# Attention phase of a ViT tower: row-maximum scores taken two steps ahead instead of one, and the work of a pair of images dealt anew over its six steps

## What is computed

```python
h = patches(x) @ W.T + b                      # 64 x 196 x 192
xn = layernorm(layernorm(h)) * g + beta
q, k, v = split(xn @ qkv_w.T + qkv_b)         # 12 heads of 16
attn = (q @ k.T) * 16 ** -0.5
attn = attn - 0.2 * (sum of the 8 neighbours of each element of attn)
h = h + softmax(attn) @ v
h = h + experts(layernorm(h))                 # top 2 of 8 experts
```

## Time and profile before

| what | value |
|---|---|
| median of 3 runs | 2177.81 us (2173.88 to 2178.31) |
| profiled execution | 2189.16 us, of which 2187.4 us from its first to its last instruction |
| attention phase | until about 1,240 us of the span |
| mean granted TensorE clock | 0.925 of full speed (2.4 GHz) |
| busy share over the span | PE 86%, DVE 67%, ACT 58%, POOL 53% |

### The profile page before, as it was taken

How to read it: one execution, slowest core, us unless ns; L and a number is a source line. 1 busy time by engine, 2 the same in 40 slices (tenths; PEclk the granted TensorE clock), 3 DMA queues, 4 the chain that set the end, 5 groups by cost and what they waited for, 6 DMA issues and landing times. The chain is left out here.

```text
span 2187.4 us, 54001 instructions
## 1 busy us (share of the span) xinstructions
PE 1891.2 (86%) x17949; PEld 1406.2 (64%) x17949; DVE 1461.1 (67%) x4652; ACT 1266.8 (58%) x2469; POOL 1152.0 (53%) x1069
## 2 busy tenths in 40 slices
PE   4758888888888989898888479999999999999991
PEld 3546666666666666666665256777777777777771
DVE  4658888888888888888887345655555555554440
ACT  3557788787878788787877323433434343333330
POOL 3335555555555545555552254666666666654452
PEclk7878999999999999999999559999999999999996
DMA  4564746666574747575664237787877878798876
GB/s 142 144 187 143 202 147 190 168 182 168 173 197 146 215 142 198 161 195 157 183 173 132 65 106 197 186 211 184 206 185 205 190 201 194 190 195 184 180 176 193
DMA packets 356572, 382.56 MB, mean 175 GB/s; under 512 B 138388, under 2 KB 319952, under 8 KB 352144
## 3 DMA queue, kind: packets, MB, share of 16 engines
q1 hardware_dynamic: 314768, 338.64, 55.3%
q0 software_dynamic: 41664, 42.12, 11.1%
HBM read 232.83 MB, written 135.46 MB: 168 GB/s over the span
## 5 line engine op out<-in xcount | busy, mean ns | idle before, releaser
L1838 ACT ACTIVATE mh<-mid_bank 128x512 bf16<-128x512 f32 x336 | 200.8, 598 | 464.0 <-PE mid_bank L1529 349.6
L824 DVE TENSOR_REDUCE row_max<-s_bank 98x2 f32<-98x392 f32 x768 | 396.6, 558 | 97.6 <-PE s_bank L607 94.7
L1750 DVE SCALAR_TENSOR_TENSOR ml<-mid_bank,mh 128x512 bf16<-128x512 f32 x336 | 231.6, 689 | 341.9 <-ACT mh L1838 333.7
L1020 ACT ACTIVATE probs<-t_bank 98x392 f32<-98x392 f32 x768 | 340.6, 498 | 42.1 <-PE t_bank L623 31.1
L1904 POOL DMA_INDIRECT sums<-y_out,tail x168 | 265.1, 1578 | 172.9 <-DVE y_out L1780 95.8
L1543 PE MATMUL y_bank<-wst,mh 128*128 128x192 bf16 x1344 | 330.0, 246 | 8.3 <-DVE y_out L1780 7.5
L1546 PE MATMUL y_bank<-wst,ml 128*128 128x192 bf16 x1344 | 330.1, 246 | 0.0
L1545 PE MATMUL y_bank<-wst,mh 128*128 128x192 bf16 x1344 | 329.8, 245 | 0.0
L623 PE MATMUL t_bank<-q_stack,k_stack 104*98 104x196 f16 x1536 | 248.6, 269 | 40.0 <-ACT probs L1020 25.5
L1193 POOL TENSOR_TENSOR x_lo<-x_buf,x_hi 128x588 f16<-128x588 f32 x128 | 188.7, 1478 | 170.6 <-ACT x_hi L1001 112.8
L1889 POOL DMA_INDIRECT slots<-row_r,spot x196 | 190.7, 973 | 98.0 <-issue 56.7
(11 more groups left out here) (236 smaller groups left out, 4515.7 us busy)
## 6 DMA issues: line engine op xcount, KB each, us to landing
wst<-packed SPq DMA_DIRECT2D x56, 1584.0 KB
x_buf<-in_x_t SPq DMA_DIRECT2D x32, 1176.0 KB, 9.0
q_stack<-stack_parts SPq DMA_DIRECT2D x96, 294.0 KB, 4.8
k_stack<-stack_parts SPq DMA_DIRECT2D x96, 294.0 KB, 6.7
stack_parts<-qk_hi SPq DMA_DIRECT2D x32, 588.0 KB, 2.9
stack_parts<-qk_lo SPq DMA_DIRECT2D x32, 588.0 KB, 2.8
sums<-h_buf SPq DMA_DIRECT2D x32, 294.0 KB
h_in<-sums SPq DMA_DIRECT2D x32, 294.0 KB
```

What stands on the lines that cost most here:

```text
L824: nc.vector.reduce_max(row_max[st.odd][:, :, hh:hh + 1], s_bank[hh % 2][0:HALF, :, 0:TOKENS], AX.X).then_inc(max_ready, 1)
L1020: nc.scalar.activation(probs[st.odd][:, hh], t_bank[hh % 2][0:HALF, :, 0:TOKENS], ACT.Exp).then_inc(probs_ready, 1)
L1750: nc.vector.scalar_tensor_tensor(ml[n % MID][:], mid_bank[n % MID_PS][:], 0.0, mh[n % MID][:], ALU.max, ALU.subtract).then_inc(ml_ready, 1)
L1838: nc.scalar.activation(mh[n % MID][:], mid_bank[n % MID_PS][:], ACT.Relu).then_inc(mh_ready, 1)
```

## The change

`scores`, `row_maxima` and `split_maxima` run two steps ahead (`LOOK = 2`); `transpose_max` and `copy_max_rows` stay one ahead, and so take maxima of the step before. The work of a pair is dealt anew: patches are multiplied in steps 0 to 2 instead of 1 and 2, and split one pair earlier; `project_v` has step 3 alone; `statistics` are in step 2, `statistics_n` in step 3, `inverse_deviation_n` in step 4; `layernorm_n` is in steps 0 and 1, `high_rows` in step 3 and `low_rows` in step 4 of the pair after the one where they were. The stacks are still made in six transfers, which the first scores of a pair wait for, now in step 4 of the pair before instead of step 5. The first two pairs are filled in interleaved, and the last pair drains over 12 steps instead of 7.

```diff
-DRAIN = STEPS + 1
+DRAIN = 2 * STEPS
+LOOK = 2
+FILL = 4
...
                 elif k == 0:
-                    load_x(Pair(body, kk, 2))
+                    load_x(Pair(body, kk, 3))
                     load_h(Pair(body, kk, -1))
-                    store_rows(Pair(body, kk, -2))
                 elif k == 1:
...
-                    for low in range(2):
-                        store_parts(Pair(body, kk, 1), low)
+                    store_parts(Pair(body, kk, 1), 0)
+                elif k == 2:
+                    store_parts(Pair(body, kk, 1), 1)
                     for low in range(2):
                         stack(Pair(body, kk, 1), low)
...
+                elif k == 5:
+                    store_rows(Pair(body, kk, -2))
...
             def step(body, kk):
-                if kk == -1:
+                if kk == -FILL:
                     fill_pipeline()
-                scores(Step(body, kk, 1), (0, 1))
+                scores(Step(body, kk, LOOK), (0, 1))
                 mix(Step(body, kk, -1))
                 transpose_back(Step(body, kk, -2))
                 scores_less_max(Step(body, kk, 0), (0, 1))
-                scores(Step(body, kk, 1), (2, 3))
+                scores(Step(body, kk, LOOK), (2, 3))
+                if kk >= 0:
+                    between_heads(body, kk)
                 scores_less_max(Step(body, kk, 0), (2, 3))
-                if kk >= 0:
-                    before_max(body, kk)
                 transpose_max(Step(body, kk, 1))
                 if kk >= 0:
-                    after_max(body, kk)
+                    after_heads(body, kk)
...
-                row_maxima(Step(body, kk, 1), (0, 1))
-                normalise(Step(body, kk, -2))
+                row_maxima(Step(body, kk, LOOK), (0, 1))
                 if kk >= 0:
...
                     elif k == 5:
                         split_low(Pair(body, kk, 2))
-                row_maxima(Step(body, kk, 1), (2, 3))
-                split_maxima(Step(body, kk, 1))
+                normalise(Step(body, kk, -2))
+                row_maxima(Step(body, kk, LOOK), (2, 3))
+                split_maxima(Step(body, kk, LOOK))
...
                 exponentials(Step(body, kk, 0), (0, 1))
-                if kk >= 0 and k < 2:
-                    high_patches(Pair(body, kk, 2), 2 * k)
+                if k >= 3:
+                    high_patches(Pair(body, kk, 3), k - 2)
+                elif k == 0:
+                    layernorm_n(Pair(body, kk, -2), (0, 1))
+                elif k == 1:
+                    take_high_tilde(Pair(body, kk, 1))
                 exponentials(Step(body, kk, 0), (2, 3))
+                copy_max_rows(Step(body, kk, 1))
...
                 elif k == 1:
-                    split_patches(Pair(body, kk, 2), (1, 2, 3))
+                    if Pair(body, kk, 1).there:
+                        pool.wait_ge(plain_lo_ready, Pair(body, kk, 1).u + 1)
                     sum_rows(Pair(body, kk, -1))
...
+                elif k > 3:
+                    split_patches(Pair(body, kk, 3), (k - 3,))
+                    if kk >= 0 and k == 4:
+                        inverse_deviation_n(Pair(body, kk, -1))
+                        low_rows(Pair(body, kk, -2))
```

More of the change, by code:

```diff
@@ L137, in run_bodies @@
 def run_bodies(eng, step):
-    step(0, -1)
+    for kk in range(-FILL, 0):
+        step(0, kk)
     for body in range(2):
@@ new lines, in fill_pipeline @@
+                pe.wait_ge(weights_in, 16 * len(LOADS))
+                pe.wait_ge(consts_set, CONSTS)
+                transpose_xn(first, 0)
+                transpose_xn(first, 1)
+                for c in range(2):
+                    project_patches(second, 0, c)
+                for i in range(BLOCKS):
+                    project_qk(first, i)
+                for c in range(2):
+                    project_patches(second, 1, c)
+                project_v(first, 0, (0, 1))
+                project_v(first, 1, (0, 1))
@@ L1007, in _ @@
             for i in range(2):
+                if i == 1:
+                    for tile in range(TILES):
+                        high_patches(Pair(0, 0, 1), tile)
                 for hh in range(HG):
```

217 lines of the change are left out of this document (110 added, 107 removed).

## The result

The changed kernel takes **2278.65 us** (median of 4 runs, 2277.55 to 2282.44), the kernel before, run again beside it, 2175.85 us (2169.55 to 2178.31): 1.048 times the time, 95% interval 1.0453 to 1.0507, or 103 us more. The forecast was 2217, at most 2275. The sign was right and the size was not.

What follows compares the result with a forecast made beforehand. Nearly full PE, DVE and ACT lose time in handing over; the change closes a loop through the stacks. Period 36.9 + 0.8 = 37.7 us, +62 over 26 periods, start -25, drain +2: +39, so 2217 us, range 2150 to 2275.

Steps and rivals of the forecast that it cites:

- The closed chain: Step 4's scores through steps 5, 0, 1, parts stored and stacks loaded to the next step 4: 36.9 us before the clock.
- 37.7 forecast: Period of a pair in the attention phase: 36.9 us of loop plus 0.8 for the clock, 2.4 more than now.
- the clock: PE's idle wait before step 4 brings half the clock, slowing step 4's matmuls: 0 to 1.6 us, taken as 0.8.
- the meeting at `split_low`: In step 5 POOL's low_rows delays DVE's split_low, so step 5 ends at 12.7 us after step 4's start, not 11.0.
- 3.0, 11.6 and 0.3: Way to the stacks: 2.9 plus 0.1 us to the first load, 11.6 of loads, 0.3 for low parts held up.
- The forecast had `sum_rows` meet `take_low_tilde` itself: sum_rows waits for take_low_plain, meets take_low_tilde and holds the low parts up by some 0.4 us: +0.3.
- it starts at 6.7 us, together with `split_low`: low_rows, behind a patch split that follows ACT's step 4 patch copy, starts 6.7 us after step 4's start; split_low at 6.8.
- All of it meets: Rival: both POOL operations between split_low's two, half clock through project_qk; period 39 to 40, at 39.5 2264 us; chance 0.12.
- an undisturbed pair: The pair whose step times the loop was summed from: 21.2 us from step 4's scores to the end of take_high_tilde.
- Together -25: The start: interleaved fill some 10 us sooner and the 17.45 us wait gone, -15; bounds -10 and -30.
- counted from the third pair on, not from the sixth: The longer period was charged from the sixth pair on: 26 periods, +62 us.
- +2: The longer drain of the last pair adds 2 us.

Runs made afterwards that it cites:

- e3: The changed kernel with its six stack loads cut into 18, six per group of four heads, step 4 waiting for its own group alone: 2218.85 us, ratio 1.021.
- e7: e6 with e4's edit, POOL's low_rows and step 5 patch split held until split_low is over: 2158.48 us, 0.988 of the kernel before.
- e8: The changed kernel with PE given 32 matmuls on the old stack, result unread, while it waits for the new one: 2308.00 us, ratio 1.054.
- e6: e3 with e5's edit, so 18 loads by group and normalise before split_low in step 5: 2215.36 us, ratio 1.013.
- e11: e6 with high_rows and low_rows in step 2, the packed weights' low parts earlier, and six whole stack loads again: 2239.39 us, ratio 1.033.
- e4: The changed kernel with POOL's low_rows and step 5 patch split held back until split_low has ended: 2276.50 us, ratio 1.048.
- e5: The changed kernel with DVE normalising before split_low in step 5: 2271.95 us, ratio 1.038.
- e1: The changed kernel with scores one step ahead instead of two (LOOK = 1), the new order kept: 2338.56 us, ratio 1.079.
- e14: e13 with scores one step ahead instead of two (LOOK = 1): 2460.03 us, 1.124 of the kernel before.
- e13: e7 with the low parts of the packed weights made earlier, in steps 3 and 4 instead of 5: 2158.55 us, ratio 0.986.

## Why the prediction was right and wrong

**Right.** The closed chain. Stacks are needed a step sooner, PE stands 3.3 to 3.7 us for them in front of step 4, the last landing comes 0.2 us before, and the loop's parts add up to the period. `max_parts` left PE's waits.

**Right by luck, the even pairs' sum.** 37.7 forecast, 38.1 measured, with step 4 at 5.7 us (forecast 4.3, and 0.8 for the clock), step 5 at 7.2 (8.4), step 0 at 4.8 (5.2), `take_high_tilde` at 4.4 (4.1) and 16.0 to the next scores (14.9). The 1.7 us of the meeting at `split_low` are in the forecast and not in the pair; what stands in their place is a longer step 4, 1.0 us at the maxima, and 1.1 on the way to the stacks. Of this last, the first load is issued 4.0 us behind `take_high_tilde`, at 763.18, right after the store of the low parts at 762.72, and the last lands 11.8 us later; I had 3.0, 11.6 and 0.3. The low parts are stored late because `take_low_tilde` starts only at 761.20, behind the maxima of step 1, and these meet POOL's `sum_rows`. DVE's timeline:

```profile
759.96 1.02 DVE L863 TENSOR_SCALAR max_parts<-row_max 98x8 f16<-98x8 f32 x1
```

And POOL's:

```profile
759.13 1.81 POOL L1239 TENSOR_TENSOR att<-att,h_in 98x768 f32<-98x768 f32 x1 [2.74 <-DVE att L882]
```

That row of DVE takes 1.02 us there in every pair from 300 to 1100 us, where it took 0.21 in the kernel before. The forecast had `sum_rows` meet `take_low_tilde` itself.

**Wrong, the meeting's place.** "it starts at 6.7 us, together with `split_low`". The forecast hung POOL's run on the patch copy that ACT makes in step 4. But POOL's split in step 4 takes the tile that ACT has copied in step 3, and so it starts as soon as POOL's layer norm of step 3 is over, in the changed kernel 0.36 us before the scores of step 4:

```profile
774.80 1.31 POOL L1224 TENSOR_TENSOR x_lo<-x_buf,x_hi 128x588 f16<-128x588 f32 x1
```

Counted from the scores that open step 3, `low_rows` starts after 12.1 us in the changed kernel (777.87 - 765.77) and after 12.2 in e3 (783.26 - 771.08). Step 4 comes 9.4 us behind step 3 with the wait for the stacks, and 5.6 without. So POOL works on while PE stands, and `low_rows` starts 2.7 us into step 4 in the changed kernel (777.87 - 775.16) and 6.6 us in e3 (783.26 - 776.64), where the forecast's 6.7 comes out by luck. The wait that I had put at the head of the chain I had not put between POOL and PE. So the run fell on the maxima of step 4, which it holds up by 2.7 us in the odd pair shown and by 1.0 in the even one. "All of it meets" at 39.5 us was the rival that came true in the odd pairs, on another row and with the half clock through `project_qk` that it had named; it had 0.12. What I had not listed at all is `pack`, a third operation in the run of every second pair; and the sum was taken from an undisturbed pair, whose step 5 took 6.06 us, while in every second pair of the kernel before it took 7.2 to 8.8. Period 39.2 instead of 37.7: 37 us over 26 periods.

**Wrong, the start.** "Together -25". The first scores came 9.6 us sooner (59.02 for 68.59), the 17.45 us wait is gone, and `take_low_tilde` of the third pair came 17.3 us sooner (117.8 for 135.1). By the sixth pair 0.8 was left. PE waited 7.83 and 4.82 us at the next two steps 4. The view names no releaser for these two waits; that they are for stacks is read from the place. In e3, where a group's scores wait for its own loads alone, they are 1.84 us and nothing, and the sixth `take_low_tilde` comes at 240.62, 10.2 us sooner than before (250.78); in e7 it comes 18.3 sooner. So the head start can't be kept when the loop through the loads is already closed, and the longer period should have been counted from the third pair on, not from the sixth: 3 x 3.9 = 11.7 of the 16.5 us that went between them. In all that is 24 us.

**The drain** was nearly right: "+2", and from the last `take_low_tilde` to the first matmul of the experts the changed kernel takes 0.9 us more (146.5 for 145.6). The other 9.6 us of the gain behind it lie in the expert phase, which the change doesn't touch and the forecast couldn't know.

37 + 24 - 1 - 10 = 50 us, and 89.8 - 39 = 51.

**The clock** can't be given a price of its own here. Step 4 took 5.7 and 4.9 us where part or all of it was granted half the clock, and 3.85 at the full clock in e8, so 0.8 was less than it took from step 4. Yet with the full clock the period rose from 39.2 to 40.1 us, since step 5 grew more than step 4 shrank. A term of its own beside the meeting can't say that.

**What the runs showed in place of the single chain** is that two causes cover each other, the late stacks and POOL's run. By group, with POOL's run at `split_low` (e6): 37.5 us. Six loads, that meeting avoided (e11): 37.6. Both faults (the changed kernel): 39.2. Neither (e7): 34.9. Moving the run alone, by e4, gave 0; with e5 and the rest of e11 it gave 1.6; the loads alone gave 1.7, and all of e7 4.3. The two edits e4 and e5 together with the six loads were not run, so the 37.6 stands on e11, which differs from e7 in more than the loads. And the look-ahead, which the change is built on, carries weight: without it the same dealing costs 3% (e1 against the changed kernel) to 14% (e14 against e13). What stays open is why the look-ahead is worth so much in the new dealing; that the projections no longer stand between PE's second scores and `transpose_max` fits, but no run tells it apart.

## What to carry to other kernels

When a change makes a transfer needed sooner, sum the closed loop through that transfer first, the meetings ahead of its stores included, and count a better start only up to the turn in which the loop closes. For every operation of a third engine in that loop look up which step's work it takes: here POOL's run was tied to step 3 and not to step 4, and so a wait of PE between the two moved it onto other rows. When an edit removes one wait and nothing happens, keep the edit and try it again with the next wait removed: here an edit worth 0 alone was worth 2.5% in company. And move short POOL operations as a run, asking which DVE rows lie beside each of them in every kind of pair, since a run that is pushed off one row lands on the next.

## What the hardware showed that I had not expected

An operation of DVE can stand through more than one operation of POOL. The first part of the maxima, one input of 98x8 elements and 0.17 us when alone, took 2.86 us and ended within 0.02 us of the third POOL operation in a row. From 300 to 1100 us of the changed kernel this row stands 121 times; 80 times it took about 0.2 us, and in the other 41 it took 1.0 to 2.9 and ended 0.03 us behind the end of a POOL operation each time. In e7 it took 1.91, past the end of `row` at 706.60 to that of `x_lo` at 707.86, and the second part then ended at 709.13, with `pack` at 709.09. The Trainium skill, "SBUF — State Buffer", section "SBUF: two separate sides", calls the port pair that DVE and GpSimd share an exclusive lock, which whichever starts first gets for the whole instruction; for DVE it names operations in a 2-port mode or with two SBUF inputs. The rows agree that the later one stands; that DVE's turn came only one or two POOL instructions further on, where the next followed without a gap, goes beyond that. The two-input `x_al` in e3 got its turn at the first boundary, where `row` ended at 784.90, and POOL's `x_lo` lost 0.3 us to it.

A stack load with a quarter of the partitions took 7.0 us from issue to use, and the whole one 8.5: four times the bytes cost 1.5 us.
